# The softmax row sums of the token stage: from ScalarE's accumulators to one VectorE sum

## The reference, cut to what matters

```python
Up = relu(x2_normed @ U_w.T)            # tokens
Uq = D_param[0] * relu(ctx @ U_w.T)     # 77 keys
scores = where(q_mask, -inf, Up @ Uq.T)
alpha = softmax(scores, axis=2)
x3 = x2 + tanh(g_xattn[1]) * (alpha @ ctx)
out = x3 + tanh(g_ffn[1]) * experts(layernorm(x3))
```

## Time and profile before

| | |
|---|---|
| median of 3 runs | 2095.22 us (2095.07 to 2097.52) |
| the profiled execution's own time | 2096.39 us |
| its span in the trace | 2094.5 us |
| mean granted TensorE clock over the span | 0.965 |
| first and last `smx` (L1087) | 169.64 and 737.56 us |
| first transfer of the expert stage's chain | 773.19 us |

### The profile page before, as it was taken

One profiled execution on the slowest core, in us unless ns is written; L12 is line 12 of the kernel. 1 busy time (PEld: TensorE's weight loads), 2 busy tenths in 40 slices (PEclk: granted clock), 3 DMA queues, 4 the chain that ended last, 5 costly groups with the idle time before them and its releaser, 6 DMA issues.

```text
span 2094.5 us, 35357 instructions
## 1 busy us (share of the span) xinstructions
PE 1948.3 (93%) x11276; PEld 1682.3 (80%) x11277; DVE 984.8 (47%) x2254; ACT 739.7 (35%) x1709; POOL 784.4 (37%) x803
## 2 busy tenths in 40 slices
PE   3579999999999828999999999999999999999997
PEld 2468887787888617989889998999898898899986
DVE  3678999899998353342411242214224114221331
ACT  2235656655656343241411132113314114211231
POOL 0565676675674133250611143114305115201250
PEclk9589999999999858999999999999999999999999
DMA  6221343443443455150610033003305104301130
GB/s 197 97 87 54 139 163 117 139 158 118 155 142 117 146 173 156 50 178 19 189 50 30 30 120 115 30 30 120 107 20 171 59 30 150 97 13 47 53 107 11
DMA packets 152260, 208.68 MB, mean 100 GB/s; under 512 B 12830, under 2 KB 78622, under 8 KB 152197
## 3 DMA queue, kind: packets, MB, share of 16 engines
q1 hardware_dynamic: 111125, 114.14, 17.2%
q10 hardware_dynamic: 25344, 50.33, 6.7%
q0 software_dynamic: 15728, 43.38, 6.6%
HBM read 140.98 MB, written 68.37 MB: 100 GB/s over the span
## 4 chain that ended last, share of the span: by engine, by line
PE 61%; ACT 0%; issue 0%; DMA 0%; POOL 0%; POOLq 0%; DVEq 0%; ACTq 0%; DVE 0%
PE bank L1742 24%; PE bank L1750 23%; PE bank L1715 6%; PE bank L1695 6%; PE bank L1673 1%; PE bank L1704 1%; DMA tg<-t_d,idx_t 0%; PE bank L1679 0%; ACT w_hi L1606 0%; ACT w_hi L1607 0%; DMA slots<-slot_d 0%; POOLq L1447 0%; POOL out_dram L1485 0%; DVEq L1388 0%; ACT inT_hi L1592 0%
## 5 line engine op out<-in xcount | busy, mean ns | idle before, releaser
L1833 DVE SCALAR_TENSOR_TENSOR hT_lo<-bank,hT_hi 128x256 fp32r<-128x256 f32 x352 | 149.1, 424 | 656.8 <-ACT hT_hi L1637 656.8
L1637 ACT ACTIVATE hT_hi<-bank 128x256 fp32r<-128x256 f32 x352 | 135.1, 384 | 747.9 <-PE bank L1742 747.9
L1742 PE MATMUL bank<-inT_hi,w_lo 128*128 128x256 f32 x1408 | 398.5, 283 | 0.0
L1742 PE MATMUL bank<-inT_lo,w_hi 128*128 128x256 f32 x1408 | 398.3, 283 | 0.0
L1742 PE MATMUL bank<-inT_hi,w_hi 128*128 128x256 f32 x1408 | 396.8, 282 | 0.0
L1485 POOL DMA_INDIRECT out_dram<-ob,idx_x x46 | 46.5, 1010 | 637.1 <-DVE ob L1843 619.7
L1750 PE MATMUL bank<-w_hi,hT_hi 128*128 128x512 f32 x704 | 279.9, 398 | 0.0
L1742 PEld LDWEIGHTS bank<-inT_hi,w_hi 128*128 128x128 f32 x1408 | 269.0, 191 | 13.3
L1742 PEld LDWEIGHTS bank<-inT_lo,w_hi 128*128 128x128 f32 x1408 | 269.0, 191 | 12.0
L1750 PE MATMUL bank<-w_lo,hT_hi 128*128 128x512 f32 x704 | 277.7, 394 | 0.0
L1750 PE MATMUL bank<-w_hi,hT_lo 128*128 128x512 f32 x704 | 274.1, 389 | 0.0
(11 more groups left out here) (303 smaller groups left out, 3988.2 us busy)
## 6 DMA issues: line engine op xcount, KB each, us to landing
stage<-in_L_ffn_W_dram SPq DMA_DIRECT2D x256, 256.0 KB, 3.5
X<-in_x_dram SPq DMA_DIRECT2D x16, 1024.0 KB, 5.2
t_d<-tt ACTq DMA_DIRECT2D x16, 1024.0 KB
x_d<-x ACTq DMA_DIRECT2D x16, 1024.0 KB, 6.7
out_dram<-y ACTq DMA_DIRECT2D x16, 1024.0 KB, 8.4
xs<-in_x_dram SPq DMA_DIRECT2D x16, 768.0 KB
cw_a<-in_L_xattn_conv_w_dram SPq DMA_DIRECT2D x2, 1024.0 KB, 17.5
cw_b<-in_L_xattn_conv_w_dram SPq DMA_DIRECT2D x2, 1024.0 KB, 19.7
```

The costliest lines, as they stand in the source:

```text
L1637: act.activation(hT_hi[:, f % 4, :], hb[f % 4][:, 0:CN], ACT.Relu).then_inc(e_hh, 1)
L1742: last = pe.matmul(hb[f % 4][:, 0:CN], l[:, k, fs], r[:, k, :], start=(n == 0), stop=(n == 3 * KB - 1))
L1833: dve.scalar_tensor_tensor(out=hT_lo[:, f % 4, :], in0=hb[f % 4][:, 0:CN], scalar=0.0, in1=hT_hi[:, f % 4, :].bitcast(F32), op0=ALU.max, o ...
```

## The change

ScalarE's four exponentials lose their accumulators. VectorE makes the four row sums itself, with one sum over `al` (128 partitions, 4 x 77 elements, from SBUF) between `alT_lo` and `srd`. The new instruction raises the semaphore v_sm, so v_sm now counts four per group and the waits on it are renumbered, and `srd` waits for the new sum.

```diff
@@ ScalarE
-                    wait(act, v_sm, 3 * d + 2)
+                    wait(act, v_sm, 4 * d + 2)
                     settled(act)
                     for j in range(T):
                         act.activation(al[:, j, :], p_sc[:, j, :], ACT.Exp, bias=nbx[:, j:j + 1],
-                                       scale=rs_c[:, ds((d % T) * T + j, 1)], accum_out=ssm[:, j:j + 1]).then_inc(a_al, 1)
+                                       scale=rs_c[:, ds((d % T) * T + j, 1)]).then_inc(a_al, 1)
@@ VectorE
                     dve.tensor_reduce(smx[:, :], p_sc[:, :, :], AX.X, ALU.max).then_inc(v_sm, 1)
-                    wait(dve, v_sm, 3 * d + 1)
+                    wait(dve, v_sm, 4 * d + 1)
@@ VectorE
                     wait(dve, a_al, T * (d + 1))
+                    dve.tensor_reduce(ssm[:, :], al[:, :, :], AX.X, ALU.add).then_inc(v_sm, 1)
+                    wait(dve, v_sm, 4 * d + 3)
                     dve.reciprocal(srd[:, :], ssm[:, :]).then_inc(v_sm, 1)
-                    wait(dve, v_sm, 3 * d + 3)
+                    wait(dve, v_sm, 4 * d + 4)
                     dve.tensor_scalar(scf[:, :], srd[:, :], gx[:, ds(d, 1)], None, ALU.mult).then_inc(v_scf, 1)
```

## The result

The changed kernel took 2099.22 us (median of 22 runs, 2096.60 to 2103.74), the kernel before 2094.81 us on the same chip (22 runs, 2092.36 to 2097.53). The ratio is 1.0023, 95% interval 1.0017 to 1.0030: slower by 0.23%, or 4.4 us, which is little, but the interval doesn't reach 1. The forecast was 2099.2 from a kernel before of 2095.22, which is +4.0.

What follows compares the result with a forecast made beforehand. A closed ring of VectorE and GpSimd was taken to bound the token stage's loop steps. Loop +4.46 and last steps -0.46 gave +4.0 on 2095.22, so 2099.2 us; 8-in-10 range 2095.0 to 2101.2.

Steps and rivals of the forecast that it cites:

- The ring: Loop steps: VectorE starts GpSimd, which holds VectorE until done; step grows from 38.66 to 39.16 us; chance 0.55.
- 1.03 of waits: VectorE's loop waits, 0.24 at `xdT_lo` and 0.79 at `up_lo`, which look like cover for the sum but aren't.
- the rival of the earlier gap: Loop steps: `lb` gets through between two GpSimd additions, one addition earlier, saving 0.22; +2.0 us, 2097.2; chance 0.12.
- (1) ScalarE: Exponentials 0.31 apart instead of 0.41, the fourth ready 0.38 us earlier; worth nothing in loop steps.
- (2) The sum: VectorE's new sum takes 0.465 us and `srd` starts 0.495 later, with bounds of 0.42 and 0.62.
- (3) Where it goes: Loop steps: the sum delays GpSimd and lengthens nine steps by 0.495 each, 4.5 us.
- if the sum takes over 0.57: Earlier gap's condition: `lb` starts 0.57 after GpSimd's second addition began, so a longer sum lets it through earlier.
- `rw` long instead of short: Profile sign in loop steps: a long `rw`, instead of `rd` ending with GpSimd's addition, means the earlier gap.
- The upper bound of 0.62: Most that the sum delays `srd`, if the wait costs 0.15; nine times it tops the ring's range, 2100.3.
- the dearer case: Sum with its wait costs 0.6 or more, or one more low-clock stretch comes; +5.1 or +6.2, 2100.9; chance 0.10.
- The low-clock step: Step 9: TensorE sets `nb_a`, VectorE has 1.8 us in hand, and the sum costs nothing.
- (4) The last steps: Steps 17 to 19: earlier fourth exponential gains 0.2 and 0.38, step 19 loses 0.12; together -0.46 us.

Runs made afterwards that it cites:

- The series of sums: Accumulators kept, unread VectorE sums added to the kernel before: 20 keys, ratio 1.0018; 50 keys, 1.0022; 50 and 77 keys, 1.0034.
- the new order: Routing's `lb` to `oh` moved ahead of the last two `xdT_lo` in loop steps: kernel before, then 2090.94 us; changed kernel, then 2091.28 us.

## Why the prediction was right

**The bound, step by step.** The ring was right: the sum is paid in a loop step although VectorE had 1.03 of waits and TensorE was busy for 97% of the time. The series of sums, and the new order in which the same sum costs nothing, show it. What came out is not the ring alone, though, which had 0.55 of the chances, but the ring with the rival of the earlier gap in it, which had 0.12.

**(1) ScalarE.** Right. The exponentials are 0.30 apart (four in 1.33), `alT_hi` is not late for anything in the loop, and taking the accumulators away alone changes no loop step. The wait of TensorE's weight loads for the first `al` did rise, to 0.89 to 0.93 in most steps, where it had been 0.61 to 0.64 (0.9 forecast).

**(2) The sum.** 0.458 us each for an estimate of 0.465, and `srd` 0.49 later. The row of `ab` was the right one to go by. The formula of the Trainium skill, "VectorE: DVE Perf Modes", section "The TRN2 errata", gave an estimate of 0.38, which is 0.08 short of the trace; the same section says itself that this formula under-predicts the duration of a single operation, which the prediction left out. What was missed is the 0.12 behind `scf`, which makes the shift 0.60.

**(3) Where it goes.** The prediction named 0.495 as the growth of a step; it is 0.39, in two mis-sized terms of opposite sign: +0.11 for the larger shift, and -0.22 for the gap, which was priced as a rival, at the right size and with the right condition ("if the sum takes over 0.57"), but held to be unlikely since only the sum itself was looked at and not the shift that GpSimd sees. `rw` long instead of short was the sign given for it. The upper bound of 0.62 and the dearer case, 0.6 or more a step, were priced at nine times 0.62 although both lie past 0.57, where the rival's own rule gives 0.22 back. Nine steps give 3.4. The low-clock step costs nothing, as forecast, though it is now step 13 (40.15; step 9 had 40.14).

**(4) The last steps.** Mis-sized: -0.46 forecast. Steps 16 to 18 together gave -0.16 (0.01, -0.10 and -0.07 for a forecast of 0, -0.2 and -0.38), and from the last `smx` to the first transfer of the expert stage's chain it is 0.10 more, about as forecast. The term that failed is above all step 18, where the sum was said to hide in VectorE's wait of 1.06 for the first product. `alT_lo` is indeed 0.36 earlier, and the first `x` too. But the second `x` is 0.15 later. VectorE in step 18 of the changed kernel:

```profile
714.51 0.75 DVE L1063 SCALAR_TENSOR_TENSOR x<-bank,scf,X 128x512 f32<-128x512 f32 x1 [0.56 <-PE bank L758]
...
715.81 0.68 DVE L1013 TENSOR_SCALAR over<-pos 128x4 f32<-128x4 f32 x1
...
716.66 0.55 DVE L1018 SCALAR_TENSOR_TENSOR fl<-fl,over 128x4 f32<-128x4 f32 x1
...
717.94 0.74 DVE L1063 SCALAR_TENSOR_TENSOR x<-bank,scf,X 128x512 f32<-128x512 f32 x1
```

`over` took 0.16 in the kernel before. The sum is ahead of `y_nb`, which starts GpSimd's `y`, and `y` now holds `over` and `fl` where it held only `fl`. With neither accumulators nor sum the second `x` comes 11.17 after `smx`, with the sum added 11.66: the sum is paid in full, by way of GpSimd. What is shown is this shift; the steps' own lengths there also depend on a clock between 0.80 and 0.85 and can't be split further.

In sum, +3.37 and -0.06 instead of +4.46 and -0.46. In the two profiles the first `smx` is 0.27 later besides, and the expert stage, which the change does not touch, is 0.17 shorter, which makes the 3.4 of the span. The median grew by 4.4, and the kernel before took 2094.81 in place of 2095.22 this time. That 2099.22 meets 2099.2 is luck: the loop term was 1.1 too large and that of the last steps 0.4 too low, the medians grew by 1.0 more than the two spans, and the kernel before was 0.4 faster than when the forecast was made.

## What to carry to other kernels

Where VectorE and GpSimd share a step, look at what stands beside each GpSimd operation before you ask how long anything is: tiny two-input operations and casts were held here for up to a whole GpSimd operation each, reductions and operations that read one tile from PSUM and one from SBUF were not. A wait on VectorE need not be cover when something behind the added work starts GpSimd; here 1.03 us of waits covered none of 0.60. If holds take turns at fixed ends, a step need not grow with the time added: work out where each held operation meets the next end (0.02 us decided it here), or better, move the held ones out from under it.

## What the hardware showed unexpectedly

A hold was decided within 0.02 us: `lb` at 1.21 to 1.25 after the additions began was through in 0.19, at 1.25 to 1.27 it took 1.32 or more. One operation got through at each end, not two. A VectorE instruction more in front of `scf` cost 0.12 beyond its duration, two more did not; no run tells why. And held operations came with a lower clock: in the kernel with the whole routing moved, `xdT_lo` kept TensorE waiting for 2.30 to 3.79 us in each of six steps, and their mean granted clock was 0.92 or 0.96; in the other six, with waits of up to 0.51, it was 1.00. In the step of 43.07 TensorE had stood still from 410.8 on when the clock fell at 412.7 from 1.00 to 0.50, the 1.2 GHz level. The kernel before has such a fall too (step 9) without a long wait, so a wait is not its only occasion.
